# A quantised feed-forward layer, its five groups and its layernorm interleaved, with clip and maxima work moved to GpSimd

## The chip, the core and the metric

The kernel runs on one core of a Trainium2 chip. A core has five engines that run their own instruction streams and meet only at semaphores: TensorE (PE in the profile, its weight loads PEld), VectorE (DVE), ScalarE (ACT), GpSimd (POOL) and SyncE (SP, which only issues DMAs here). The metric is the time of one execution in microseconds (us); lower is better. TensorE, VectorE and ScalarE reach PSUM, the matmul accumulators of 8 banks; all engines reach SBUF.

## The reference

`x` is 16 images of 96 channels by 256 pixels. It passes, each time added to a residual, through two convolution-like attention layers (L0, L1), a causal attention (L2), a quantised feed-forward layer (`L2_ffn`), a causal attention (L3) and a mixture of experts (`L3_ffn`). The change is in the quantised feed-forward layer and in the layernorms; this is that layer:

```
h   = layernorm(x)                       # over the 96 channels of each token
y1  = h @ binarized(W1).T + b1           # 96 -> 384, weights are signs about a group mean
y1  = quantise(y1)                       # per group of 3 images
y1  = gelu(y1)
y2  = y1 @ binarized(W2).T + b2          # 384 -> 96
y2  = quantise(y2)
x   = x + y2

quantise(y), for g in range(5):          # images 3g, 3g+1, 3g+2; the 16th image stays zero
    gamma = max(abs(y[g]))               # one number over the whole group
    y[g]  = clip(y[g] * 128 / (gamma + 1e-5), -128 + 1e-5, 128 - 1e-5)
```

The scale of a group needs the maximum over all its elements, so nothing of a group can pass the gelu before the last element of its first product is there, and nothing can be added to `x` before the last of its second.

## The kernel before

Tokens are 4096, in 32 tiles of 128. `tok` holds the residual with tokens on partitions, `on` the normalised copy, `xn` the same with channels on partitions (TensorE's transposes turn one into the other, four tiles, called a chunk, at a time; 8 chunks). `big` (called `y1` here) holds the hidden layer, `ps` is PSUM. A group has 768 tokens, computed as two halves of 384.

**Layernorm** (`layer_norm` on VectorE, `norm_tail` on ScalarE, `normed_to_channels` on TensorE), used four times as `ln2`, `lnf2`, `ln3`, `lnf3`: VectorE takes statistics, ScalarE a square root, VectorE the reciprocal; then of each chunk VectorE normalises three tiles and ScalarE one (`on`), TensorE transposes the four, and ScalarE copies the result into `xn`.

**The feed-forward stage** follows an order written out by hand in three tables. `h` is the first matmul of a group (six products of 128x384, one PSUM bank each), `c` ScalarE's copies of them to `y1`, `a` VectorE's maximum of absolute values along each partition, `q` scale and clip of `y1` on VectorE, `e` the gelu on ScalarE, `y` on TensorE the second matmul and on VectorE the addition of the bias and the maximum, `f` scale, clip, addition to `tok`, and the statistics of the next layernorm. After each `a` and each `y` GpSimd takes the maximum over the partitions (`partition_all_reduce`). The first matmul starts when all eight chunks of the layernorm are in `xn`. `quant_scale` turns a maximum into a scale with three small VectorE steps, each waited for (`link`).

```
F2_PE  = ["h0", "h1", "h2", "h3", "y0", "h4", "y1", "y2", "y3", "y4"]
F2_ACT = ["c0", "c1", "c2", "e0", "c3", "e1", "c4", "e2", "e3", "e4"]
F2_DVE = ["a0", "a1", "q0", "a2", "q1", "a3", "q2", "y0", "a4", "q3", "y1", "f0", ...
```

Each engine takes its steps strictly in its table's order, so a step that waits holds up everything behind it.

Of the kernel before, what the change touches and what calls it, by code (L numbers as in the profile page):

```python
# [60 lines left out]
NORM = {"gn0": 1, "gn1": 2, "ln2": 3, "lnf2": 4, "ln3": 5, "lnf3": 6}  # L61
TURN = {"ln2": 0, "lnf2": 8, "ln3": 16, "lnf3": 24}
# [19 lines left out]
def hybrid_kernel(nc, x_d, w96_d, w128_d, out_d):  # L82
    ctx = ExitStack()
    with ctx:
# [162 lines left out]
        def _(pool):  # L247
# [30 lines left out]
            for l in (1, 2, 3):  # L278
                pool.wait_ge(sg("w96_loaded"), 16)
                if l == 1:  # L280
# [40 lines left out]
        def _(act):  # L321
# [7 lines left out]
            def norm_tail(name):  # L329

                norm_sqrt(name, P, NT)
                act.wait_ge(sg("norm_scale"), TURN[name] // 8 + 1)
                for g in range(9):
                    if g < 8:
                        t = 4 * g + 3
                        nc.scalar.activation(on[:, t, :], tok[:, t, :], ACT.Identity, bias=st[:, 6, t:t + 1],  # L336
                                             scale=st[:, 5, t:t + 1]).then_inc(sg("ln_ta"), 1)
                    if g >= 1:
                        act.wait_ge(sg("ln_t_ps"), TURN[name] + g)
                        nc.scalar.activation(xn[0:C, (g - 1) * 512:g * 512], ps[0:C, 4 + (g - 1) % 4, :], ACT.Copy).then_inc(sg("xn_copied"), 1)  # L340
# [7 lines left out]
            act.wait_ge(sg("l0_logit"), 1)  # L348
            nc.scalar.activation(aff[:, :, :], a0[:, :, :], ACT.Exp, scale=C ** -0.5).then_inc(sg("l0_exp"), 1)
            nc.scalar.activation(st[:, 5, :], st[:, 4, :], ACT.Exp, scale=-C ** -0.5).then_inc(sg("l0_exp"), 1)  # L350
            act.wait_ge(sg("l0_qkv_ps"), 1)
            nc.scalar.activation(qkv0[:, :, :], ps[0:C, 2, 0:3 * B * M].rearrange("p (a b) -> p a b", a=3), ACT.Copy).then_inc(sg("l0_qkv"), 1)
            act.wait_ge(sg("l0_sc"), 1)
            nc.scalar.activation(pr2[:, :, :, :], pr[:, :, :, :], ACT.Exp, scale=(C // H0) ** -0.5).then_inc(sg("l0_sexp"), 1)
            act.wait_ge(sg("l0_proj_ps"), 1)
            nc.scalar.activation(s64[:, 5, :], ps[0:C, 0, 0:B * M], ACT.Identity, bias=wa("l0_pb", C)).then_inc(sg("l0_stf2"), 1)
            act.wait_ge(sg("l0_stft_ps"), 1)
            nc.scalar.activation(stft[:, :], ps[0:B * M, 1, 0:C], ACT.Copy).then_inc(sg("l0_stft"), 1)
# [43 lines left out]
            for l in (1, 2, 3):  # L402
# [38 lines left out]
                if l == 2:  # L441
# [10 lines left out]
                    norm_tail("lnf2")  # L452
                    act.sem_inc(sg("f2_y1"), 6)
# [778 lines left out]
```

## Time and profile before

| | |
|---|---|
| time, median of 3 runs | 1001.02 us (998.97 to 1004.37) |
| profiled execution, first to last instruction | 1000.7 us |
| TensorE busy | 826.8 us (83%) |
| VectorE busy | 733.6 us (73%) |
| ScalarE busy | 586.7 us (59%) |
| GpSimd busy | 138.3 us (14%) |
| mean granted TensorE clock | 0.918 of full speed |
| the feed-forward stage, from its layernorm's scale to the last statistics | 554.85 to 630.49 us |

A time in the trace counts from the first instruction. The profiled execution's own time is its span, 1000.7 us; nothing lies around it in the numbers given, and it stands 0.3 us below the median of the runs. A row of the timeline gives start, length, engine, line of the kernel, operation, what is written and read, how many instructions it merges, and in brackets how long the engine had been idle and who released it. Instructions of one engine overlap a little at their ends, so the pitch from one start to the next, not the length, is what an engine spends.

### The profile page before, as it was taken

What the parts mean: (1) busy time and instruction counts of PE and PEld (TensorE: products, weight loads), DVE (VectorE), ACT (ScalarE), POOL (GpSimd) and SP (SyncE); (2) the same over time, 40 slices, a digit from 0 to 9 for tenths busy, and PEclk for the clock granted to TensorE, in tenths of its full rate; (3) what the DMA queues carried; (4) which work ended last, traced back from release to release, by engine and by line L of the source; (5) the groups of instructions that cost most, each with busy time, mean ns of one, the idle gap of its engine ahead of it and who ended that gap; (6) DMA issues with size and microseconds to landing.
All of it is one profiled execution on the core that took longest, in us unless ns stands there. A gap on an engine that the chain in (4) does not pass through costs nothing.

```text
span 1000.7 us, 19812 instructions
## 1 busy us (share of the span) xinstructions
PE 826.8 (83%) x5997; PEld 667.3 (67%) x5997; DVE 733.6 (73%) x2103; ACT 586.7 (59%) x1826; POOL 138.3 (14%) x200
## 2 busy tenths in 40 slices
PE   0875799999999466999997776489999949999996
PEld 0761566666666364778885456278788738999995
DVE  6317799999999653899998599479999972354344
ACT  0211678777777224888887652378889842444442
POOL 9002333333333000000000000000000010000000
PEclk9997899999999776999999797679999967999998
DMA  5000000000000643566664000246666600000000
GB/s 187 1 0 1 1 0 0 0 0 0 0 0 0 57 70 48 90 85 94 94 94 63 1 0 1 32 78 85 91 94 94 91 4 1 9 8 16 8 8 16
DMA packets 51260, 38.05 MB, mean 38 GB/s; under 512 B 28448, under 2 KB 43296, under 8 KB 50976
## 3 DMA queue, kind: packets, MB, share of 16 engines
q1 hardware_dynamic: 50784, 36.14, 23.8%
q0 software_dynamic: 448, 1.57, 0.6%
q8 instruction: 14, 0.23, 0.1%
q14 instruction: 14, 0.11, 0.0%
HBM read 6.24 MB, written 3.15 MB: 9 GB/s over the span
## 4 chain that ended last, share of the span: by engine, by line
PE 65%; DVE 22%; issue 5%; DMA 4%; SPq 2%; ACT 2%; DVEq 0%; ACTq 0%
PE ps L660 9%; PE ps L790 8%; PE ps L610 8%; PE ps L769 7%; PE ps L557 6%; PE ps L564 6%; DVE sqj L995 3%; PE ps L601 3%; PE ps L566 3%; DVE ee L958 2%; PE ps L574 2%; PE ps L575 2%; DVE on L856 2%; DVE chst L837 2%; DVE xn L831 2%
## 5 line engine op out<-in xcount | busy, mean ns | idle before, releaser
L380 ACT ACTIVATE ee<-ps,nmax 128x128 f32<-128x128 f32 (+1 forms) x588 | 248.9, 442 | 10.2 <-DVE nmax L917 7.7
L958 DVE TENSOR_SCALAR ee<-ee,rrec 128x128 f32<-128x128 f32 (+1 forms) x588 | 173.4, 358 | 5.2
L660 PE MATMUL ps<-w,ee 128*128 128x128 f32 x960 | 137.3, 280 | 19.7 <-DVE ee L958 19.7
L367 ACT ACTIVATE big<-ps 128x384 f32<-128x384 f32 (+1 forms) x224 | 113.3, 538 | 40.4 <-PE ps L660 39.5
L660 PEld LDWEIGHTS ps<-w,ee 128*128 128x128 f32 x960 | 104.2, 142 | 45.3 <-DVE ee L958 33.7
L380 ACT ACTIVATION_READ_ACCUMULATOR ee<-ps,nmax 128x1 f32 x588 | 124.1, 211 | 0.0
L917 DVE TENSOR_REDUCE nmax<-ps 128x2 f32<-128x256 f32 x200 | 101.1, 546 | 18.1 <-PE ps L566 18.1
L564 PE MATMUL ps<-qk 128*128 128x128 f32 (+1 forms) x400 | 103.8, 349 | 12.6 <-DMA qk<-lo 9.6
L471 ACT ACTIVATE big<-ps 128x512 f32<-128x512 f32 x96 | 57.3, 597 | 84.5 <-PE ps L769 83.2
L790 PEld LDWEIGHTS ps<-w,big 128*128 128x128 f32 x768 | 98.1, 191 | 7.1
L564 PEld LDWEIGHTS ps<-qk 128*128 128x128 f32 x400 | 79.9, 207 | 30.6 <-issue 17.1
L557 PE MATMUL ps<-kh,big 128*128 128x256 f32 x400 | 97.4, 387 | 1.6 <-ACT ee L380 1.6
L275 POOL TENSOR_TENSOR big<-qs,w 96x256 f32<-96x256 f32 x108 | 78.6, 758 | 144.6 <-ACT qs L390 144.6
L790 PE MATMUL ps<-w,big 128*128 128x96 f32 x768 | 96.3, 272 | 0.0
L610 PE MATMUL ps<-big,vh 128*32 128x256 f32 (+1 forms) x1188 | 92.4, 353 | 0.5 <-DVE big L989 0.5
L566 PE MATMUL ps<-maskb,identb 128*128 128x128 bf16 x400 | 90.4, 236 | 0.0
L769 PE MATMUL ps<-qk 128*128 128x512 f32 x288 | 88.1, 423 | 1.0 <-DVE gate L1118 1.0
L557 PEld LDWEIGHTS ps<-kh,big 128*128 128x128 f32 x400 | 74.3, 192 | 17.7 <-issue 6.2
L1152 DVE TENSOR_TENSOR big<-ps,w 128x384 f32<-128x384 f32 x32 | 15.6, 550 | 87.8 <-PE ps L790 87.8
L914 DVE TENSOR_REDUCE nmax<-ps 128x4 f32<-128x1024 f32 x50 | 60.9, 1217 | 17.4 <-PE ps L557 17.4
L269 POOL COPY xb<-xn 96x256 f32 (+1 forms) x54 | 24.8, 462 | 327.1 <-PE ps L587 277.4
L495 PE MATMUL ps<-w,on 128*96 128x128 f32 x128 | 29.9, 411 | 42.8 <-ACT on L336 27.1
(215 smaller groups left out, 1296.4 us busy)
## 6 DMA issues: line engine op xcount, KB each, us to landing
qk<-hi SPq DMA_DIRECT2D x36, 192.0 KB, 3.7
qk<-hi SPq DMA_DIRECT2D x72, 96.0 KB, 3.8
qk<-lo SPq DMA_DIRECT2D x36, 192.0 KB, 4.8
qk<-lo SPq DMA_DIRECT2D x72, 96.0 KB, 4.6
w<-w_in SPq DMA_DIRECT2D x1, 1829.5 KB, 13.9
xc<-x_in SPq DMA_DIRECT2D x4, 384.0 KB, 5.9
l_mix<-on SPq DMA_DIRECT2D x8, 192.0 KB, 6.5
tok<-l_mix POOLq DMA_DIRECT2D x4, 384.0 KB, 4.9
```

Source lines behind the costliest of these rows:

```text
L275: last = nc.gpsimd.tensor_tensor(qh[0:C, par, g, :], qs[:, :], wa("l1_hw", C)[:, g:g + 1].broadcast_to([C, N]), ALU.mult)
L367: nc.scalar.activation(et[:, h, 0:w], ps[:, 4 + hh, 0:w], ACT.Copy).then_inc(own(l, f"et{hh}"), 1)
L380: last = nc.scalar.activation(ee[:, ke, hh, qc, 0:w], src, ACT.Exp, bias=nmax[:, kp, hh, qc:qc + 1], accum_out=rsum[:, kp, hh, qc:qc + 1])
L557: last = mm(ps[:, 2 * kp + hh, qc * N:(qc + 1) * N], qh[:, par, 2 * u + hh, qc * P:(qc + 1) * P], kh[:, par, :], start=True, stop=True)
L564: mm(ps[:, 2 * kp + hh, qc * N:qc * N + w], qk[:, par, h, 0, qc * P:(qc + 1) * P], qk[:, par, h, 1, 0:w], start=True, stop=False)
L566: last = mm(ps[:, 2 * kp + hh, qc * N + qc * P:qc * N + (qc + 1) * P], identb[:, :], maskb[:, :], start=False, stop=True)
L610: last = mm(ps[32 * r:32 * (r + 1), 6, g * N + q0:(g + 1) * N], vh[:, par, tc, 3 * g + r, :], et[:, 3 * g + r, tc * N:tc * N + N - q0], st ...
L660: last = nc.tensor.transpose(ps[:, 4 + hh, b * P:(b + 1) * P], ee[:, u, hh, qc, tc * P:(tc + 1) * P], ident)
L769: last = mm(ps[:, 4 + s % 4, :], w1hl[:, w, s * P:(s + 1) * P], xhl[:, par, x, :], start=(n == 0), stop=(n == 2))
L790: last = mm(ps[:, q, e * C:(e + 1) * C], h3[:, r % 4, q * P:(q + 1) * P], wb("f3_w2")[:, r * C:(r + 1) * C], start=(j == 0), stop=(j == NJ ...
L917: last = V.tensor_reduce(out=nmax[:, kp, :, qc], in_=ps[:, 2 * kp:2 * kp + 2, qc * N:qc * N + scores_cols(l, qc)], axis=AX.X, op=ALU.max, ...
L958: last = V.tensor_scalar(v, v, rrec[:, kp, hh, qc:qc + 1], None, ALU.mult)
```

## The change

- **Tables.** `F2_PE`, `F2_ACT` and `F2_DVE` are new, and GpSimd gets one of its own, `F2_POOL`. The eight chunks of the `lnf2` layernorm are steps in them (`t` on TensorE, `m` and `x` on ScalarE), put between the half-groups of the first matmul. A half-group waits for the chunk that holds its last token. The transposes of `lnf2` use PSUM banks 6 and 7 in place of 4 to 7.
- **Scale in the gelu.** `q` no longer touches `y1`. It is one reciprocal on VectorE, and ScalarE's gelu multiplies by that scale. The gelu runs in halves.
- **Clip after the gelu**, on GpSimd (`p`), in halves, as one instruction with two operations. The second matmul waits for the clip of its half.
- **Maxima.** After each all-reduce GpSimd adds the epsilon and divides by 128 itself, a second small instruction; VectorE keeps the reciprocal.
- **Layernorm.** In `ln2`, `lnf2`, `ln3` and `lnf3` one more tile of each chunk moves, from VectorE to GpSimd (`norm_pool`): two tiles on VectorE, one on GpSimd, one on ScalarE.
- **Semaphores of layer L0** are merged into three, counted up; the order of work there is the same.

```diff
-F2_PE = ["h0", "h1", "h2", "h3", "y0", "h4", "y1", "y2", "y3", "y4"]
-F2_ACT = ["c0", "c1", "c2", "e0", "c3", "e1", "c4", "e2", "e3", "e4"]
-F2_DVE = ["a0", "a1", "q0", "a2", "q1", "a3", "q2", "y0", "a4", "q3", "y1", "f0", "q4", "y2", "f1", "y3", "f2", "y4", "f3", "f4"]
+F2_PE = ["t0", "h00", "t1", "h01", "t2", "h10", "t3", "h11", "t4", "h20", "t5", "h21", "t6", "t7",
+         "y0", "h30", "h31", "y1", "h40", "h41", "y2", "y3", "y4"]
+F2_ACT = ["m0", "m1", "x0", "c00", "m2", "x1", "c01", "m3", "x2", "c10", "m4", "x3", "c11", "m5", "x4", "e00", "e01",
+          "c20", "m6", "x5", "c21", "m7", "x6", "x7", "e10", "e11", "e20", "e21", "c30", "c31", "e30", "e31",
+          "c40", "c41", "e40", "e41"]
+F2_DVE = ["a0", "q0", "a1", "q1", "a2", "y0", "q2", "f0", "a3", "y1", "q3", "f1", "a4", "y2", "q4", "f2", "y3", "f3", "y4", "f4"]
+F2_POOL = ["a0", "p0", "a1", "p1", "a2", "y0", "p2", "a3", "y1", "p3", "a4", "y2", "p4", "y3", "y4"]
...
+            def norm_pool(name):
+
+                pool.wait_ge(sg("norm_scale"), TURN[name] // 8 + 1)
+                for g in range(8):
+                    t = 4 * g + 2
+                    nc.gpsimd.tensor_scalar(on[:, t, :], tok[:, t, :], st[:, 5, t:t + 1], st[:, 6, t:t + 1], ALU.mult, ALU.add).then_inc(sg("ln_tp"), 1)
...
+                        if step[0] == "p":
+                            for b in range(2):
+                                v = y1[:, :, g * GT + b * (GT // 2):g * GT + (b + 1) * (GT // 2)]
+                                pool.wait_ge(sg("f2_gelu"), 2 * g + b + 1)
+                                nc.gpsimd.tensor_scalar(v, v, QB - QEPS, -QB + QEPS, ALU.min, ALU.max).then_inc(sg("f2_clip"), 1)
+                        else:
...
+                            nc.gpsimd.partition_all_reduce(m, amax[:, 2 * k, g:g + 1], P, bass.bass_isa.ReduceOp.max).then_inc(sg(f"f2_gred{k}"), 1)
+                            pool.wait_ge(sg(f"f2_gred{k}"), g + 1)
+                            nc.gpsimd.tensor_scalar(m, m, QEPS, 1.0 / QB, ALU.add, ALU.mult).then_inc(sg(f"f2_gmax{k}"), 1)
...
-                            act.wait_ge(sg("f2_quant"), g + 1)
-                            nc.scalar.activation(y1[:, :, g * GT:(g + 1) * GT], y1[:, :, g * GT:(g + 1) * GT], ACT.Gelu).then_inc(sg("f2_gelu"), 1)
+                            act.wait_ge(sg("f2_scale"), g + 1)
+                            nc.scalar.activation(y1[:, :, c0:c1], y1[:, :, c0:c1], ACT.Gelu, scale=amax[:, 0, g:g + 1]).then_inc(sg("f2_gelu"), 1)
...
+                bank, banks = (6 + g % 2, 2) if name == "lnf2" else (4 + g % 4, 4)
...
+                            pe.wait_ge(sg("xn_copied"), TURN["lnf2"] + (a + GT // 2 - 1) // 512 + 1)
...
-                            pe.wait_ge(sg("f2_gelu"), g + 1)
                             for b in range(2):
+                                pe.wait_ge(sg("f2_clip"), 2 * g + b + 1)
...
-                            quant_scale(0, g)
-                            v = y1[:, :, g * GT:(g + 1) * GT]
-                            link(V.tensor_scalar(v, v, amax[:, 0, g:g + 1], QB - QEPS, ALU.mult, ALU.min))
-                            V.tensor_scalar(v, v, -QB + QEPS, None, ALU.max).then_inc(sg("f2_quant"), 1)
+                            dve.wait_ge(sg("f2_gmax0"), g + 1)
+                            V.reciprocal(amax[:, 0, g:g + 1], amax[:, 1, g:g + 1]).then_inc(sg("f2_scale"), 1)
...
-                            quant_scale(1, g)
+                            dve.wait_ge(sg("f2_gmax1"), g + 1)
+                            link(V.reciprocal(amax[:, 2, g:g + 1], amax[:, 3, g:g + 1]))
```

VectorE's rows at steps `a4 q3 y1 f0` of the kernel before: the maximum of group 4 along partitions, the three small steps and the two passes over the hidden layer of group 3 (`big`), the second layer's bias and maximum of group 1 (`on`), and the first small steps of group 0's last part.

```order
L1079 TENSOR_REDUCE amax<-big 128x1
L1071 TENSOR_SCALAR amax<-amax 128x1
L1072 RECIPROCAL amax<-amax 128x1
L1073 TENSOR_SCALAR amax<-amax 128x1
L1084 TENSOR_SCALAR big<-big,amax 128x3x768
L1085 TENSOR_SCALAR big<-big 128x3x768
L1092 TENSOR_TENSOR on<-ps,w 128x288 x2
L1095 TENSOR_REDUCE amax<-on 128x1
L1071 TENSOR_SCALAR amax<-amax 128x1
```

The same engine at steps `a3 y1 q3 f1` of the change:

```order
L1122 TENSOR_REDUCE amax<-big 128x1
L1133 TENSOR_TENSOR on<-ps,w 128x288 x2
L1136 TENSOR_REDUCE amax<-on 128x1
L1126 RECIPROCAL amax<-amax 128x1
L1140 RECIPROCAL amax<-amax 128x1
L1142 TENSOR_SCALAR on<-on,amax 128x576
L1143 SCALAR_TENSOR_TENSOR tok<-on,tok 128x576
```

The two passes over `big` are gone, and `f` of a group (L1140 on) now follows the maximum of the same group (L1136) with one reciprocal between them; before, `f` used the maximum of the group ahead.

GpSimd before, through the whole feed-forward stage:

```order
L290 COMPARE_AND_BRANCH
L316 ISA
L316 ISA amax<-amax 128x1 x10
L269 COPY xb<-xn 96x256 x2
L290 UNCONDITIONAL_BRANCH
```

GpSimd after, from the layernorm `lnf2` to step `p1` (L340 is the all-reduce, L342 the small step behind it, L335 the clip):

```order
L278 TENSOR_SCALAR on<-tok,st 128x96 x8
L340 ISA
L340 ISA amax<-amax 128x1
L342 ISA
L342 TENSOR_SCALAR amax<-amax 128x1
L335 TENSOR_SCALAR big<-big 128x3x384 x2
L340 ISA
L340 ISA amax<-amax 128x1
L342 ISA
L342 TENSOR_SCALAR amax<-amax 128x1
L335 TENSOR_SCALAR big<-big 128x3x384 x2
```

An all-reduce now stands behind the clips of another group on the same engine, and each has a second instruction behind it.

## Rows read from the trace of the kernel before

**Rows 1.** Windows: length; busy us of PE, PEld, DVE, ACT, POOL; clock; DMA

```profile
554.80:580.00 25.20, 22.86 (x79) 14.28 (x80) 14.95 (x33) 17.52 (x35) 0.73 (x2) 0.82 0.00 1
580.00:600.00 20.00, 14.49 (x86) 11.94 (x84) 19.55 (x21) 10.94 (x15) 1.40 (x4) 0.91 0.00 0
```

**Rows 2.** Timeline of VectorE in the feed-forward stage

```profile
554.85 5.85 DVE L856 TENSOR_SCALAR on<-tok,st 128x96 f32<-128x96 f32 x24
569.46 2.55 DVE L1079 TENSOR_REDUCE amax<-big 128x1 f32<-128x2304 f32 x1 [8.76 <-ACT big L460]
...
576.36 1.82 DVE L1084 TENSOR_SCALAR big<-big,amax 128x2304 f32<-128x2304 f32 x1
578.21 1.76 DVE L1085 TENSOR_SCALAR big<-big 128x2304 f32<-128x2304 f32 x1
579.89 2.54 DVE L1079 TENSOR_REDUCE amax<-big 128x1 f32<-128x2304 f32 x1
...
601.04 0.81 DVE L1092 TENSOR_TENSOR on<-ps,w 128x288 f32<-128x288 f32 x2
601.88 0.75 DVE L1095 TENSOR_REDUCE amax<-on 128x1 f32<-128x576 f32 x1
602.55 0.14 DVE L1071 TENSOR_SCALAR amax<-amax 128x1 f32<-128x1 f32 x1
...
603.12 0.52 DVE L1100 TENSOR_SCALAR on<-on,amax 128x576 f32<-128x576 f32 x1
...
606.11 0.15 DVE L1071 TENSOR_SCALAR amax<-amax 128x1 f32<-128x1 f32 x1
...
622.26 0.75 DVE L1095 TENSOR_REDUCE amax<-on 128x1 f32<-128x576 f32 x1
...
626.48 0.15 DVE L1071 TENSOR_SCALAR amax<-amax 128x1 f32<-128x1 f32 x1
...
630.49 0.18 DVE L848 TENSOR_SCALAR st<-chmv 128x32 f32<-128x32 f32 x1
```

**Rows 3.** Timeline of ScalarE in the same stage

```profile
577.18 1.28 ACT L464 ACT_TABLE_LOAD   x1
580.00 2.12 ACT L464 ACTIVATE big<-big 128x2304 f32<-128x2304 f32 x1 [1.54 <-DVE big L1085]
582.03 2.38 ACT L460 ACTIVATE big<-ps 128x384 f32<-128x384 f32 x6
```

**Rows 4.** Timeline of TensorE in the same stage (a matmul is two records)

```profile
555.72 1.94 PE L495 MATMUL ps<-w,on 128*96 128x128 f32 x8 [9.65 <-ACT on L336]
...
564.76 15.75 PE L740 MATMUL ps<-xn,w 128*128 128x384 f32 x48 [0.68 <-ACT xn L340]
582.27 4.23 PE L753 MATMUL ps<-w,big 128*128 128x96 f32 x36 [1.76 <-ACT big L464]
...
601.63 7.38 PE L753 MATMUL ps<-w,big 128*128 128x96 f32 x36 [2.21 <-DVE on L1092]
```

**Rows 5.** Window inside the last of these rows, columns as Rows 1

```profile
602.00:604.00 2.00, 2.00 (x11) 2.00 (x11) 1.86 (x6) 1.28 (x1) 0.35 (x1) 0.50 0.03 8
```

**Rows 6.** Timeline of GpSimd, its nearest operations

```profile
572.15 0.38 POOL L316 PARTITION_ALL_REDUCE amax<-amax  x1 [41.83 <-DVE amax L1079]
...
802.63 1.46 POOL L308 CAST qk<-w 128x1536 fp32r<-128x1536 f32 x1 [13.66 <-DMA qk<-lo]
811.56 2.89 POOL L310 TENSOR_TENSOR qk<-w,qk 128x1536 fp32r<-128x1536 f32 x1 [7.47 <-issue]
```

**Rows 7.** Timeline of VectorE and GpSimd where they work together

```profile
811.53 2.99 DVE L856 TENSOR_SCALAR on<-tok,st 128x96 f32<-128x96 f32 x1
...
142.48 1.14 DVE L958 TENSOR_SCALAR ee<-ee,rrec 128x256 f32<-128x256 f32 x4
...
144.54 4.45 POOL L275 TENSOR_TENSOR big<-qs,w 96x256 f32<-96x256 f32 x6 [8.63 <-ACT qs L390]
...
147.41 2.12 DVE L958 TENSOR_SCALAR ee<-ee,rrec 128x256 f32<-128x256 f32 x4
```

More of the change, by code:

```diff
@@ L485, in group_sums, with normed_chunk @@
                 mm(ps[0:C, 0, B:2 * B], wb("avg3", C), st[0:C, 1, 0:B], start=True, stop=True).then_inc(sg("gn_vg"), 1)
+            def normed_chunk(name, g):
+                bank, banks = (6 + g % 2, 2) if name == "lnf2" else (4 + g % 4, 4)
+                pe.wait_ge(sg("ln_tn"), TURN[name] + g + 1)
+                pe.wait_ge(sg("ln_tp"), TURN[name] + g + 1)
+                pe.wait_ge(sg("ln_ta"), TURN[name] + g + 1)
+                if g >= banks:
+                    pe.wait_ge(sg("xn_copied"), TURN[name] + g - banks + 1)
+                for t in range(4):
+                    last = nc.tensor.transpose(ps[0:C, bank, t * P:(t + 1) * P], on[:, g * 4 + t, :], ident)
+                last.then_inc(sg("ln_t_ps"), 1)
             def normed_to_channels(name):
                 for g in range(8):
[L490 to L496 removed]
+                    normed_chunk(name, g)
             pe.wait_ge(sg("w128_loaded"), 16)
@@ L734, in _ @@
                         g = int(step[1])
-                        if step[0] == "h":
-                            for b in range(2):
-                                for j in range(NJ):
-                                    a = g * GT + b * (GT // 2)
-                                    pe.wait_ge(sg("f2_y1"), g * 6 + (b * NJ + j + 1))
-                                    mm(ps[:, b * NJ + j, 0:GT // 2], wa("f2_w1")[:, j * P:(j + 1) * P], xn[:, a:a + GT // 2],
-                                       start=True, stop=True).then_inc(sg("f2_y1_ps"), 1)
+                        if step[0] == "t":
+                            normed_chunk("lnf2", g)
+                        elif step[0] == "h":
+                            b = int(step[2])
+                            a = g * GT + b * (GT // 2)
+                            pe.wait_ge(sg("xn_copied"), TURN["lnf2"] + (a + GT // 2 - 1) // 512 + 1)
+                            for j in range(NJ):
+                                pe.wait_ge(sg("f2_y1"), g * 6 + (b * NJ + j + 1))
+                                mm(ps[:, b * NJ + j, 0:GT // 2], wa("f2_w1")[:, j * P:(j + 1) * P], xn[:, a:a + GT // 2],
+                                   start=True, stop=True).then_inc(sg("f2_y1_ps"), 1)
                         else:
@@ L854, in layer_norm @@
                 for g in range(8):
-                    for t in range(4 * g, 4 * g + 3):
+                    for t in range(4 * g, 4 * g + 2):
                         last = V.tensor_scalar(on[:, t, :], tok[:, t, :], st[:, 5, t:t + 1], st[:, 6, t:t + 1], ALU.mult, ALU.add)
```

151 lines of the change are left out of this document (77 added, 74 removed).

## The prediction, made before the changed kernel was run

> **What bounds the kernel now.** I read the page first: TensorE is busy most, but the chain that ended last passes through both TensorE and VectorE, and the change touches one stage, so I went to that stage's timeline. It starts at 554.85, when the layernorm's scale is ready and VectorE begins on its 24 tiles, and ends at 630.49, when the statistics of the next layernorm are done [rows 2]: 75.6 us. Outside it the change only moves one tile per chunk in three other layernorms. The reader should see three things. First, from 554.8 to 580 VectorE is busy 14.95 of 25.2 us, and one wait of 8.76 us before the first maximum is most of the rest [rows 1, 2]; TensorE is busy 22.86 us of the same stretch, at a mean clock of 0.82. Second, from 580 on VectorE is the engine that never stops, 19.55 of 20 us [rows 1], while TensorE waits for it [rows 4]. Third, GpSimd does next to nothing here, 1.40 us of those 20.
>
> So the stage splits at the start of the third maximum, `a2`, at 579.89 [rows 2]: before it TensorE's feed of hidden-layer products sets the pace, behind it VectorE's own work, 50.6 us of it. I work out the two parts apart.
>
> **First part, up to `a2`.** The interleaving lets TensorE begin the first matmul after one chunk instead of eight. What that brings depends on the clock. Before, TensorE starts its transposes at 555.72, eight of them in 1.94 us, 0.24 each [rows 4]; when the first matmul starts at 564.76 it takes 15.75/24 = 0.66 us per product of 384 columns. The mean clock of 0.82 over the stretch, against the two levels of 0.5 and 1.0, says that the first 9 us of it ran at the lower level, 1.2 GHz. The new order puts products of twice 0.66 = 1.3 us into these 9 us. From 555.7: chunk 0 (four transposes) 0.96, its copy with two signals 0.8, `h00` 3.9, chunk 1 0.96, its copy 0.8, one product of `h01` 1.3, together 8.7, which is 564.4. Then at the full clock: two products 1.3, chunk 2 0.6, its copy 0.8, `h10` 2.0, chunk 3 0.6, `h11` 2.0, which ends at about 571.6, and its last copy at 572.2. Copies are 2.38/6 = 0.40 us per 384 columns [rows 3], so about 0.5 for a chunk of 512. From there ScalarE's table is the chain: tile and copy (`m5`, `x4`) 0.9, the table load of 1.28, two half gelus of 1.2 each (half of 2.12 and 0.14 more for the second start), `c20` 1.2, `m6` and `x5` 0.9, `c21` 1.2 [rows 3], together 7.9. So `a2` starts at 580.1, 0.2 us later than before. The early start is spent on the lower clock and on the table load and gelu that now stand ahead of group 2's copies. What is ahead, though, is the work behind: `q0` and `q1` no longer cost VectorE anything that it has not idle time for.
>
> **Second part, from `a2` on.** VectorE's pitches before [rows 2]: `a` 2.45, `y` 601.04 to 602.55 = 1.51, three small steps 602.55 to 603.12 = 0.57, `f` without them 603.12 to 606.11 = 2.99 (0.45 more for the last, of eight tiles), `q` 0.57 + 1.85 + 1.68 = 4.1. Three `a` 7.4, four `q` 16.4, five `y` 7.6, five `f` with small steps 17.8 + 0.45, waits 1.0: 50.6, which is the trace. After: 7.4, three reciprocals at 0.2 = 0.6, 7.6, and five `f` with one reciprocal 16.0 + 0.45, together 32.0. That takes off 18.6 us. Four things give some back:
>
> - **The second layer of group 0 (3.0 us).** `y0` follows `a2` at 582.5 at once, but TensorE can only start it at about 581.9, after the last chunk's copy, and needs 4.23 for it [rows 4]; VectorE waits until about 586.2, 0.4 of which is its own addition. I take 3.0; at 1.8 for a half it would be 2.6.
> - **Round trips of the maxima (4.9 us).** Before, another step always lay between a maximum and its use. Now `q` stands right behind, and `f` one reciprocal behind. A round trip is a signal to GpSimd (a maximum ending at 572.01 releases it at 572.15: 0.14), the all-reduce (0.35 to 0.38), a signal, the small step, a signal. I take the small step no longer than the all-reduce, so 3 x 0.14 + 2 x 0.35 = 1.1 us [rows 2, 6]. It is seen five times, three of them with 0.2 of reciprocal over it: 3 x 0.9 + 2 x 1.1 = 4.9. Queued behind VectorE's wait is all the rest of the stage. The trace bounds the trip from above only loosely: from the maximum ending at 623.01 to its use at 626.48, 3.47 us [rows 2].
> - **GpSimd and VectorE in each other's way (4.2 us).** A VectorE tile that took 0.24 in pitch elsewhere took 2.99 us when a GpSimd operation of 2.89 us ran beside it, until that ended; four others took 2.12 instead of 1.14 [rows 6, 7]. So GpSimd holds VectorE's SBUF-to-SBUF `tensor_scalar` for its own length. `f0`, `f1` and `f2` have such an instruction (0.52) and one that reads two SBUF operands, and the clips of groups 2, 3 and 4 fall beside them: a clip follows the gelu that follows `q`, and `f` follows `q` too. A clip is 128x1152. At the cast's rate, 1.46/1536, it is 1.1 us; at that of the two-operand operation, 2.89/1536, 2.2 [rows 6]. It has one tensor operand, as the cast, and two operations, so I take 1.4. One clip per `f` in the way: 3 x 1.4 = 4.2.
> - **TensorE at the lower clock (1.3 us).** After gaps of some 4 us, a group's second layer took 7.38 in place of 4.23 us at a clock of 0.50 [rows 4, 5]. `y3` and `y4` get such gaps ahead of them. Most of `y3` hides under `f2`; of `y4` one slow half less cover remains, 1.3.
>
> Together 13.4. The second part falls by 18.6 - 13.4 = 5.2.
>
> The Trainium skill, "SBUF — State Buffer", section "Who interferes with whom", says that GpSimd shares one pair of SBUF ports with VectorE as an exclusive lock held for a whole instruction, taken by VectorE's two-port modes and, for reads, by its instructions with two SBUF inputs. Rows 7 agree for the two-port case; by the rule the addition into `tok` is held as well, which the trace does not show alone. By that rule at its hardest, both of a group's clips would hold `f`, 8.4 us in place of 4.2.
>
> **The layernorm tiles, nothing (0.3 either way, each of four).** VectorE needs 5.85/24 = 0.24 per tile; a chunk of three costs it 0.73, of two 0.49. TensorE takes 0.97 per chunk plus its waits, so it is the slower, and VectorE's saving is under it [rows 2, 4]. A GpSimd tile of 96 columns costs between nothing measurable and 0.4, and even if both take turns a chunk is ready in 0.9. Without that cover, a GpSimd tile over 0.6, each layernorm loses some 8 x 0.1. In `lnf3` the tiles queue behind the 2.89 us operation of rows 6, which holds VectorE there already. The merged semaphores of L0 wait for the same things in the same order: nothing.
>
> **Sum.** First part +0.2, second part -5.2: the profiled 1000.7 becomes 995.7, the median 1001.0 becomes 996.0.
>
> **The rivals.**
>
> - *GpSimd is cheap.* The casts and copies come near this; nothing holds `f`, because the clips slip into `f`'s statistics, and a round trip is 0.8. It gives back 4.2 + 1.5 more: 990.3. Against it stand rows 7.
> - *The round trip is long (slower).* The 0.35 us of an all-reduce is one engine's record; before, no one waited for it within 3.47 us [rows 2, 6], so nothing shows what it costs a waiter. Each further us costs five exposures at `f`, and the two all-reduces that stand ahead of each of three clips on GpSimd push these into `f` as well: 8 us per us. It decides at 1.1 + 5.0/8 = 1.7 us; at 2.6 the time is 1008, at the bound of 3.47 it is 1015. "Perfetto Trace Analysis" of the Trainium skill, section "GPSIMD Engine Instruction", says that such spans are not to be trusted and that one should go by spacing; here the spacing is silent up to 3.47.
> - *The gain is eaten on GpSimd (no change).* GpSimd's operation at 811.56 had been idle for 7.47 us while VectorE ran its statistics, though its input was ready at 804.1 [rows 6]. If statistics keep GpSimd out, three clips wait 1.3 us each for the end of `f`, and with a clip of 2.2 us in place of 1.4 three more times 0.8 is lost: together 6.3, which gives 1002; one of the two alone gives 998.4 to 1000.
> - *The early start pays after all.* If TensorE reached its full clock 4 us sooner, with matmuls in place of transposes, the first part would shrink by 2 us: 994.
>
> The Trainium skill's "GPSIMD Engine Reference", section "Engine selection", advises against elementwise work on GpSimd, about twice as slow with two inputs and near VectorE's rate with one. Rows 6 show both, 1.88 and 0.95 ns per element; the clip is of the second kind.
>
> **Chances.** My forecast with the early-start variant, 992 to 999: 0.50, of which 0.29 lies more than 0.5% (5 us, about what a measurement of this kernel tells from no change) below the median. Cheap GpSimd: 0.15. Eaten gain, 998 to 1004: 0.14. Long round trip: 0.21, of which 0.18 is slower by over 0.5%. Faster: 0.29 + 0.15 = 0.44. Slower: 0.18 and 0.02 for a clip and a trip both dear. The rest, 0.36, is within 0.5%. The range takes in the cheap case with 2 us for a better first part, 988, and reaches to a round trip of about 2.6, 1008.
>
> **What would show it.** Each step has its row: `a2`'s start near 580 (first part); VectorE's idle time before the reciprocals of L1126 and L1140, 0.9 to 1.1 us each (round trip); L1142 or L1143 at 1.5 us or more with a clip beside it (hold); L335 near 1.4 us; the second layers of groups 3 and 4 at a clock of 0.5; unchanged starts of the first transposes after the layernorms. I am wrong if L1126 and L1140 wait 2 us, if L335 is over 2 us, or if `a2` starts before 577.

## The result, and the profile after

The changed kernel takes 1088.58 us, median of 4 runs (1086.16 to 1090.9); the kernel before, on the same chip, 1001.01 (998.97 to 1004.37). The ratio is 1.0867, 95% interval 1.084 to 1.0894: 87.6 us slower, where the prediction had 5 us faster and a range that ended at 1008. The profiled execution took 1088.56 us, with a span of 1086.5.

Almost all of it is in the feed-forward stage. It now runs from 555.37 to 716.98 us, 161.6 us, where it took 75.6 [rows 2]: 86.0 us more. The windows of the stage after, with the columns of [rows 1], say at once which kind of loss it is:

```profile
554.80:580.00 25.20, 17.11 (x60) 10.07 (x60) 9.62 (x21) 15.82 (x31) 6.63 (x12) 0.84 0.00 0
580.00:600.00 20.00, 16.43 (x92) 13.58 (x92) 4.10 (x5) 5.30 (x9) 2.85 (x4) 0.80 0.00 1
600.00:717.00 117.00, 26.62 (x121) 22.91 (x120) 32.04 (x97) 13.03 (x19) 11.84 (x22) 0.58 0.00 0
```

From 600 on no engine is busy more than 28% of the time: VectorE 32.04 of 117 us, TensorE 26.62, GpSimd 11.84. VectorE never stopped before (19.55 of 20 us); now it stands idle most of the time. So no engine's work is the limit: the engines wait for something that is not the length of an instruction. The waits of VectorE (engine, what waits, for whom: us in total, times, the longest) name it:

```profile
DVE amax L1140 <- POOL amax L342: 59.2, 5, 13.6
DVE amax L1126 <- POOL amax L342: 49.7, 5, 14.3
```

These are the two uses of a maximum, the scale of `f` (L1140) and that of the gelu (L1126). Ten waits hold 108.9 us. The prediction counted five of them as seen, 0.9 to 1.1 us each, 4.9 us together. The waits of GpSimd itself:

```profile
POOL amax L342 <- issue: 71.2, 10, 7.9
...
POOL amax L340 <- issue: 47.0, 8, 6.0
```

"issue" is idle time in which the engine waited for no other engine that the profile shows. GpSimd's timeline shows where in the work of a group it lies (L340 is the all-reduce, L342 the small step on its result, L335 the clips):

```profile
568.43 0.38 POOL L340 PARTITION_ALL_REDUCE amax<-amax  x1 [9.22 <-DVE amax L1122]
575.57 0.18 POOL L342 TENSOR_SCALAR amax<-amax 128x1 f32<-128x1 f32 x1 [6.75 <-issue]
577.32 2.29 POOL L335 TENSOR_SCALAR big<-big 128x1152 f32<-128x1152 f32 x2 [1.57 <-ACT big L507]
585.30 0.38 POOL L340 PARTITION_ALL_REDUCE amax<-amax  x1 [5.69 <-issue]
592.46 0.18 POOL L342 TENSOR_SCALAR amax<-amax 128x1 f32<-128x1 f32 x1 [6.79 <-issue]
...
624.01 0.18 POOL L342 TENSOR_SCALAR amax<-amax 128x1 f32<-128x1 f32 x1 [7.21 <-issue]
624.27 2.46 POOL L335 TENSOR_SCALAR big<-big 128x1152 f32<-128x1152 f32 x2
```

```profile
632.65 0.38 POOL L340 PARTITION_ALL_REDUCE amax<-amax  x1 [5.92 <-issue]
640.23 0.18 POOL L342 TENSOR_SCALAR amax<-amax 128x1 f32<-128x1 f32 x1 [7.21 <-issue]
646.16 0.38 POOL L340 PARTITION_ALL_REDUCE amax<-amax  x1 [5.75 <-issue]
653.42 0.18 POOL L342 TENSOR_SCALAR amax<-amax 128x1 f32<-128x1 f32 x1 [6.88 <-issue]
653.68 2.46 POOL L335 TENSOR_SCALAR big<-big 128x1152 f32<-128x1152 f32 x2
```

The small step of 0.18 us starts 7 us after the all-reduce of 0.38 whose result it takes. The next all-reduce starts 6 us after the `tensor_scalar` ahead of it. Between one clip and that of the next group (624.27 to 653.68, 29.4 us) these four gaps are 5.92 + 7.21 + 5.75 + 6.88 = 25.8 us. Two `tensor_scalar` in a row (L342, then L335 at 624.27) have no gap. A passage from the all-reduce to `tensor_scalar` or back is called a turn from here on. What lies in the gaps shows when one asks for everything that is recorded on a line, the small step's line L342 here (operation, count, shortest/median/longest ns, first and last start):

```profile
L342 POOLq MODIFY_POOL_CONFIG  x20: 82/83/83, 568.8 to 705.9; - x20
L342 POOL TENSOR_SCALAR amax<-amax x10: 181/181/182, 575.6 to 713.1; 128x1 f32<-128x1 f32 x10
```

Ten `tensor_scalar` and, in GpSimd's queue, a `MODIFY_POOL_CONFIG` ahead of each (two records for each), the first at 568.8, as soon as the all-reduce is done. L340 has 20 such records as well. This is the nameless `ISA` row that stands ahead of each L340 and each L342 in the order shown with the change; before, the whole stage had one.

VectorE's timeline after, to be read against [rows 2]:

```profile
575.78 0.16 DVE L1126 RECIPROCAL amax<-amax 128x1 f32<-128x1 f32 x1 [7.48 <-POOL amax L342]
575.86 2.53 DVE L1122 TENSOR_REDUCE amax<-big 128x1 f32<-128x2304 f32 x1
592.68 0.16 DVE L1126 RECIPROCAL amax<-amax 128x1 f32<-128x1 f32 x1 [14.28 <-POOL amax L342]
592.76 2.53 DVE L1122 TENSOR_REDUCE amax<-big 128x1 f32<-128x2304 f32 x1
...
624.22 0.16 DVE L1140 RECIPROCAL amax<-amax 128x1 f32<-128x1 f32 x1 [13.64 <-POOL amax L342]
624.42 1.31 DVE L1142 TENSOR_SCALAR on<-on,amax 128x576 f32<-128x576 f32 x1
625.76 1.58 DVE L1143 SCALAR_TENSOR_TENSOR tok<-on,tok 128x576 f32<-128x576 f32 x1
```

`a2` starts at 592.76 instead of 580.1, behind the first two long waits. A wait that has both turns in it, into the all-reduce and out of it, is 13.0 to 14.3 us.

**Theories, stated before the experiments.** Theory 1: GpSimd has to load other code whenever it goes from the all-reduce to `tensor_scalar` or back, 6 to 7 us each time, and nothing else matters. The rivals: the all-reduce's result reaches a waiter late, some 7 us, whatever follows it; or GpSimd is overloaded or held out by VectorE, having clips and maxima in one in-order queue. The expectations below number them theories 2 and 3; neither gives a price to a small GpSimd instruction that nobody waits for.

### The profile page after: what moved, and what is told of

Same layout as the page of the kernel before. It is cut to its first block, busy times and chain, and to the rows that moved or that the text cites. A ratio compares the mean times of both kernels' runs of the same rounds, so it can differ in the third digit from the quotient of the medians.

```text
span 1086.5 us, 19879 instructions
## 1 busy us (share of the span) xinstructions
PE 831.3 (77%) x5997; PEld 669.1 (62%) x5997; DVE 708.9 (65%) x2041; ACT 587.0 (54%) x1831; POOL 167.5 (15%) x252
## 4 chain that ended last, share of the span: by engine, by line
PE 59%; DVE 16%; issue 14%; DMA 4%; ACT 2%; SPq 2%; POOL 1%; DVEq 0%; POOLq 0%; ACTq 0%
PE ps L709 8%; PE ps L841 8%; PE ps L659 7%; PE ps L820 7%; PE ps L606 6%; PE ps L613 5%; DVE sqj L1046 3%; PE ps L650 2%; PE ps L615 2%; DVE ee L1009 2%; DMA qk<-lo 2%; PE ps L623 2%; PE ps L624 2%; DVE xn L882 2%; SPq L236 1%
## 5 line engine op out<-in xcount | busy, mean ns | idle before, releaser
L709 PEld LDWEIGHTS ps<-w,ee 128*128 128x128 f32 x960 | 104.1, 142 | 45.4 <-DVE ee L1009 33.5
L841 PE MATMUL ps<-w,big 128*128 128x96 f32 x768 | 96.4, 272 | 0.0
L804 PE MATMUL ps<-w,big 128*128 128x96 f32 x180 | 30.3, 348 | 57.6 <-DVE on L1133 56.7
L539 PE MATMUL ps<-w,on 128*96 128x128 f32 x128 | 27.0, 368 | 57.7 <-POOL on L278 39.1
```

The source lines that it names most:

```text
L709: last = nc.tensor.transpose(ps[:, 4 + hh, b * P:(b + 1) * P], ee[:, u, hh, qc, tc * P:(tc + 1) * P], ident)
L841: last = mm(ps[:, q, e * C:(e + 1) * C], h3[:, r % 4, q * P:(q + 1) * P], wb("f3_w2")[:, r * C:(r + 1) * C], start=(j == 0), stop=(j == NJ ...
```

## The experiments

In each batch the kernel before ran on the same chip; the ratio is to that, over all runs, and can differ a little from the quotient of the two medians. Each diff is cut to the lines that matter.

**1. Half the turns.** The small step goes back to VectorE, so that a group has two turns (into its maxima, back to its clips) in place of four.

```diff
-    nc.gpsimd.partition_all_reduce(...).then_inc(sg(f"f2_gred{k}"), 1)
-    pool.wait_ge(sg(f"f2_gred{k}"), g + 1)
-    nc.gpsimd.tensor_scalar(m, m, QEPS, 1.0 / QB, ALU.add, ALU.mult).then_inc(sg(f"f2_gmax{k}"), 1)
+    nc.gpsimd.partition_all_reduce(...).then_inc(sg(f"f2_gmax{k}"), 1)
 (VectorE, "q" and ahead of "f")
+    link(V.tensor_scalar(m, m, QEPS, 1.0 / QB, ALU.add, ALU.mult))
```

> The changed kernel, with the small step behind each all-reduce given back to VectorE; the clips stay on GpSimd. Theory 1 (GpSimd must load other code whenever it goes from an all-reduce to a tensor_scalar or back, about 6 to 7 us each, seen as a pool-configuration row and idle time with the releaser issue): the turns in the feed-forward stage fall from 20 to 10, a period of one group falls from 29 to some 17 us, and the time to 1015 to 1040. Theory 2 (an all-reduce itself takes 7 us to finish, whatever stands beside it): all ten remain and the time stays above 1075. Theory 3 (the new order of steps makes engines wait, GpSimd's code is no part of it): within 5 us of 1088.

Measured: 1028.71 us (1028.16 to 1036.02), ratio 1.0277 (1.0234 to 1.032). Two thirds of the loss (59.9 of 87.6 us) went. GpSimd's queue has twelve loads where the change has twenty: two in place of four in each group, and the last one ahead of the tiles of `ln3`. What is left stands where it did, now ahead of the clip:

```profile
584.81 0.38 POOL L340 PARTITION_ALL_REDUCE amax<-amax  x1 [5.82 <-issue]
592.34 2.25 POOL L335 TENSOR_SCALAR big<-big 128x1152 f32<-128x1152 f32 x2 [7.15 <-issue]
```

**2. No turns inside the groups.** In addition the clips are on VectorE (steps `p`), so that GpSimd does all-reduces alone; the interleaving of the groups, the gelu's scale and the layernorm tiles stay.

```diff
-F2_POOL = ["a0", "p0", "a1", "p1", "a2", "y0", "p2", ...]
+F2_POOL = ["a0", "a1", "a2", "y0", "a3", "y1", "a4", "y2", "y3", "y4"]
-F2_DVE = ["a0", "q0", "a1", "q1", "a2", "y0", "q2", "f0", ...]
+F2_DVE = ["a0", "q0", "a1", "q1", "p0", "a2", "p1", "y0", "q2", "f0", "p2", ...]
```

> As the first, and the clips go to VectorE too, with steps p in its table; GpSimd does nothing but all-reduces between the layernorm and the next. Interleaving, scale inside the gelu and moved layernorm tiles stay. Theory 1: no turn is left inside the stage, waits of VectorE for GpSimd fall under 1.5 us, and the stage takes 55 to 68 us in place of 161.6: 982 to 996. Theory 2: ten all-reduces of 7 us, most of them waited for: above 1040. Theory 3: the order is kept, so the time stays near 1080.

Measured: 1002.97 us (999.48 to 1005.89) against 1003.06, ratio 1.0004 (0.9988 to 1.0021). The loss is gone, but the gain that was expected did not come: the range was 982 to 996. In GpSimd's timeline one turn is left, from the last all-reduce to the layernorm tile of `ln3`:

```profile
621.96 0.35 POOL L340 PARTITION_ALL_REDUCE amax<-amax  x1 [5.11 <-DVE amax L1140]
629.43 3.62 POOL L278 TENSOR_SCALAR on<-tok,st 128x96 f32<-128x96 f32 x8 [7.11 <-issue]
```

VectorE's tiles of this layernorm started at 627.26, so GpSimd's came 2.2 us behind them, and TensorE's first transpose started at 630.02, 2.76 us behind them. Experiment 5 takes this up.

**3 and 4. The turn alone.** To the kernel before, with its order and its engines, one GpSimd instruction of 128x1 on unused memory is added behind each all-reduce. Nobody waits for it. In one kernel it is a `tensor_scalar`, in the other a `tensor_copy`.

```diff
     nc.gpsimd.partition_all_reduce(...).then_inc(sg(f"f2_gmax{k}"), 1)
+    nc.gpsimd.tensor_scalar(junk[:, x:x + 1], junk[:, 0:1], 1.0, 1.0, ALU.add, ALU.mult)   # 3
+    nc.gpsimd.tensor_copy(junk[:, x:x + 1], junk[:, 0:1])                                  # 4
```

> The kernel before, with one tensor_scalar of 128x1 on GpSimd added behind each all-reduce, on a column that nothing else uses and nobody waits for. Theory 1: ten more turns each way, about 13 us from one all-reduce to the next where 2.5 to 9.2 us were, and the stage grows by 60 to 80 us: 1060 to 1085. Theories 2 and 3: no change, 999 to 1004, since nothing waits for the new operation.

> The kernel before, with a tensor_copy of 128x1 in the place of that tensor_scalar. In both traces copies follow an all-reduce or a tensor_tensor without a pool-configuration row. Theory 1: copies belong to the code that is always there, so no change: 999 to 1004. If any other operation between two all-reduces costs the turn, 1060 to 1085 as with the tensor_scalar.

Measured: with the `tensor_scalar` 1068.04 us (1066.04 to 1068.74), ratio 1.0639 (1.0616 to 1.0661); with the copy 1002.84 (998.41 to 1005.36), ratio 0.9996 (0.998 to 1.0012). Ten instructions of 0.18 us that nobody needs cost 65 us, ten of 0.25 us nothing. GpSimd's timelines, the `tensor_scalar` first:

```profile
571.63 0.38 POOL L316 PARTITION_ALL_REDUCE amax<-amax  x1 [41.63 <-DVE amax L1080]
579.16 0.18 POOL L318 TENSOR_SCALAR junk<-junk 128x1 f32<-128x1 f32 x1 [7.15 <-issue]
585.41 0.38 POOL L316 PARTITION_ALL_REDUCE amax<-amax  x1 [6.06 <-issue]
```

```profile
568.38 0.38 POOL L316 PARTITION_ALL_REDUCE amax<-amax  x1 [41.73 <-DVE amax L1080]
568.65 0.25 POOL L318 COPY junk<-junk 128x1 f32<-128x1 f32 x1
572.22 0.35 POOL L316 PARTITION_ALL_REDUCE amax<-amax  x1 [3.32 <-DVE amax L1080]
```

GpSimd has hardly more work than before in either kernel, and nearly the same in both, so overload falls with the pair. A late result of the all-reduce can't be it either: nobody waits for one here, and where VectorE waits for it directly, in experiment 2, it is idle for 0.22 to 0.55 us. Nor is it GpSimd's wait on its own semaphore between the two instructions, which the change added: experiment 3 has no such wait and the same gap, experiment 7 has the wait and no gap. What the runs show is that the gap depends on the kinds of the two instructions; that it is code being loaded is read from the record's name.

**5. The last turn out of the way.** Experiment 2 with the third tile of `ln3` back on VectorE, and the turn taken by a `tensor_scalar` for which nobody waits, in the idle time behind the last all-reduce.

```diff
-                if l > 1:
-                    norm_pool(f"ln{l}")
+                if l == 2:
+                    norm_pool("ln2")
+                if l == 3:
+                    nc.gpsimd.tensor_scalar(junk[:, 250:251], wb("mask")[:, 0:1], 1.0, 1.0, ALU.mult, ALU.mult)
 (VectorE)
-                    for t in range(4 * g, 4 * g + 2):
+                    for t in range(4 * g, 4 * g + (3 if name == "ln3" else 2)):
```

> The maxima-only version (clips and small steps on VectorE, one all-reduce kind on GpSimd) with the third layernorm tile of every chunk of ln3 back on VectorE, so that no GpSimd instruction stands between the last all-reduce and TensorE's first transpose. One tensor_scalar of 128x1 that nobody waits for takes the load for the tiles of lnf3 in the idle time behind it. Theory 1 (loading GpSimd's code on each change between all-reduce and tensor_scalar): the wait of TensorE on L278, which ended 2.2 us behind the scale, goes, and the time falls by about 2 us against the maxima-only version, to 999 to 1001.5. Rival (the gain of the interleaving is lost elsewhere, in the colder clock of TensorE after the stage): no change against it, 1002 to 1004.

Measured: 997.5 us (996.03 to 999.27) against 1003.7, ratio 0.995 (0.993 to 0.997), somewhat better than expected and the fastest complete kernel of the study. GpSimd's timeline behind the last all-reduce:

```profile
621.49 0.35 POOL L343 PARTITION_ALL_REDUCE amax<-amax  x1 [5.10 <-DVE amax L1143]
628.53 0.19 POOL L298 TENSOR_SCALAR junk<-w 128x1 f32<-128x1 f32 x1 [6.69 <-issue]
```

The gap is the same 7 us, but TensorE's transposes start at 627.65, 0.86 us behind the start of VectorE's tiles (626.79) in place of 2.76. That is 1.9 us for the turn. The medians of experiments 2 and 5 lie 5.5 us apart, and the other 3.6 are not shown to come from it: the two ran in different batches, and the parts of the kernel that no edit touches move by as much. The kernel before and experiments 3, 4 and 10, the same code up to there, started the stage's tiles between 551.2 and 554.9. From the first tile of `lnf2` to that of `ln3` this kernel's trace has 75.1 us, experiment 2's 71.7 and the kernel before 76.7, so what the interleaving itself gains, 1.6 to 5.0 us by these traces, is uncertain too.

**6. No clips.** Experiment 1 without the clip of the gelu's result.

```diff
-                                nc.gpsimd.tensor_scalar(v, v, QB - QEPS, -QB + QEPS, ALU.min, ALU.max).then_inc(sg("f2_clip"), 1)
 (TensorE)
-                                pe.wait_ge(sg("f2_clip"), 2 * g + b + 1)
+                                pe.wait_ge(sg("f2_gelu"), 2 * g + b + 1)
```

> The changed kernel with the small step on VectorE and without the clip of the gelu's result (left out), so GpSimd does all-reduces alone from group 0 to the last. Theory 1: no turn of code lies inside the groups any more, so nothing waits for GpSimd beyond 0.6 us, VectorE does 32 us of work behind a2 plus waits of about 6 us for the second layer of group 0 and the round trips, and the last turn costs 2 us at ln3: 986 to 994. Rival (the all-reduce's round trip itself is long when VectorE waits at once for it, 3 us or more each): 1005 to 1015.

Measured: 998.9 us (996.27 to 1003.81), ratio 0.9964 (0.9946 to 0.9983). The rival's 1005 to 1015 is out, but the expectation of 986 to 994 was missed too. It had counted VectorE's work and left out that VectorE waits for ScalarE in each of groups 3 and 4 (1.26 us); experiment 7 shows the same loop more clearly. The turn ahead of `ln3`, which was expected, is there (GpSimd idle for 7.00 us).

**7. The change with one kind of code.** Every all-reduce is replaced by a `tensor_scalar`; nothing else is touched. The kernel leaves out the maximum over the partitions.

```diff
-                            nc.gpsimd.partition_all_reduce(m, amax[:, 2 * k, g:g + 1], P, bass.bass_isa.ReduceOp.max).then_inc(...)
+                            nc.gpsimd.tensor_scalar(m, amax[:, 2 * k, g:g + 1], 1.0, 1.0, ALU.mult, ALU.mult).then_inc(...)
```

> The changed kernel with every all-reduce of the two maxima replaced by a tensor_scalar of 128x1, which leaves out the maximum over the partitions; clips, small steps, waits, steps and their order are those of the change. All of GpSimd's work in the stage is now of one kind. Theory 1: no loads at all, the idle time ahead of L342 and of the replaced instruction falls from 6 to 8 us to under 0.3, and the whole loss goes: 988 to 1000, where the prediction had 996; a clip of 1.2 us with an f beside it still holds VectorE's tensor_scalar for some 0.8 us twice a group. Rival (GpSimd's in-order queue of 15 steps with clips ahead of reductions is a good part of the loss, whatever its code): 1015 or more.

Measured: 993.85 us (992.95 to 994.19) against 1003.7, ratio 0.9906 (0.9882 to 0.9929). All clips, small steps, waits and orders of the change are in it, and it is 9.9 us faster than before instead of 87.6 slower. GpSimd's timeline, the same places as in the changed kernel above:

```profile
578.15 0.19 POOL L340 TENSOR_SCALAR amax<-amax 128x1 f32<-128x1 f32 x1
578.43 0.19 POOL L342 TENSOR_SCALAR amax<-amax 128x1 f32<-128x1 f32 x1
583.62 2.29 POOL L335 TENSOR_SCALAR big<-big 128x1152 f32<-128x1152 f32 x2 [5.00 <-ACT big L507]
...
592.83 2.77 POOL L335 TENSOR_SCALAR big<-big 128x1152 f32<-128x1152 f32 x2 [0.89 <-ACT big L507]
```

No "issue" time is left. This kernel also lets the other terms of the prediction be read one by one, below.

**8. The layernorm tiles alone.** The kernel before with the third tile of each chunk on GpSimd (`norm_pool`, and its wait on TensorE), nothing else.

> The kernel before with one part of the change alone: the third layernorm tile of every chunk on GpSimd. Theory 1: three turns of code come with it. The one ahead of the first all-reduce and the one between the last all-reduce and ln3 fall into idle time (6.8 us from the last all-reduce to the scale in the kernel before, against a load of 7), so at most 1 us is lost there; in lnf3 the code is loaded already for the subtraction behind it, which starts earlier and no longer holds the tiles of VectorE, 2.5 us gained: 998 to 1001.5, against 1001 to 1003 for the kernel before. Rival (elementwise work on GpSimd slows the layernorms): 1003 to 1008, half a us or more lost in each of four.

Measured: 1000.61 us (999.36 to 1003.33) against 1003.7, ratio 0.9982 (0.9967 to 0.9997), as expected: 3.1 us faster by the medians, 1.8 by the ratio. The subtraction follows its cast at once (805.41 behind 803.86), and the tiles of `ln3` on GpSimd end their wait with the scale, not with "issue".

**9. Bound inside the scale.** Experiment 6 made into a complete kernel, with the `ln3` arrangement of experiment 5. In place of the clip, the 128x1 scale is bounded, by one small VectorE instruction more in each group, so that no scaled value passes 128 - eps.

```diff
+                            link(V.tensor_scalar(amax[:, 0, g:g + 1], amax[:, 1, g:g + 1], QEPS, 1.0 / QB, ALU.add, ALU.mult))
+                            link(V.scalar_tensor_tensor(out=amax[:, 1, g:g + 1], in0=amax[:, 1, g:g + 1], scalar=1.0 / (QB - QEPS), in1=amax[:, 0, g:g + 1], op0=ALU.mult, op1=ALU.max))
```

> The version without clips, small step on VectorE, made into a full kernel: the bound that the clip kept is put into the 128x1 scale (the greater of (m + eps)/128 and m/(128 - eps) is inverted, so no scaled value passes 128 - eps), and the third layernorm tile of ln3 is on VectorE with the load for lnf3 taken behind the last all-reduce, as in e5. Theory 1 (turns of code) with TensorE as the pace of the groups: against e6 the wait for the last turn, 2 us, and the slowed tiles of VectorE beside it, 1 us, go: 995 to 997, below e5's 997.5 by 0.5 to 2, since a group takes 9.1 us with TensorE as the pace and 9.6 with VectorE. Rival (VectorE and TensorE alternate so tightly that one 128x1 instruction more per group shows each time): 997 to 999, no better than e5.

Measured: 998.96 us (995.02 to 1000.86) against 1002.64, ratio 0.9963 (0.9947 to 0.9979): not better than experiment 5, as the rival had it. A group takes 9.33 us (594.67 to 604.00) in its trace, against 9.14 in experiment 6 and 9.63 in experiment 5: the small instruction shows its 0.19 us in each. The expectation took TensorE for the pace; in the trace VectorE waits for ScalarE (1.41 us a group). What keeps the time up beyond that stays open; the expected 0.5 to 2 us are within the spread of its runs.

**10. The turn taken early, in the kernel before.** One `tensor_scalar` of 128x1 behind the last all-reduce, for which nobody waits.

```diff
         (behind the loop over the all-reduces)
+                    nc.gpsimd.tensor_scalar(junk[:, 250:251], wb("mask")[:, 0:1], 1.0, 1.0, ALU.mult, ALU.mult)
```

> The kernel before with one instruction more: a tensor_scalar of 128x1 on GpSimd behind the last all-reduce, for which nobody waits. Theory 1: it takes the load of GpSimd's code in idle time (the next work of GpSimd comes 18 us later), so the subtraction that follows the cast near 803 starts at once instead of 7.5 us later and no longer lies beside the 24 layernorm tiles of lnf3, which take 5.8 us in place of 8.5: 2 to 3 us faster than the kernel before, and no MODIFY_POOL_CONFIG idle time ahead of the subtraction. Rival (the 7.5 us are GpSimd held out by VectorE's statistics, as the prediction read them): nothing changes.

Measured: 999.48 us (997.02 to 1001.34) against 1002.64, ratio 0.9977 (0.9964 to 0.9991): one useless instruction gains 3.2 us by the medians, 2.3 by the ratio. The subtraction of [rows 6] follows its cast at once, and VectorE's 24 tiles take 5.84 us where they took 8.51 before (and one of them 2.99, [rows 7]):

```profile
798.62 1.46 POOL L308 CAST qk<-w 128x1536 fp32r<-128x1536 f32 x1 [13.81 <-DMA qk<-lo]
800.17 2.90 POOL L310 TENSOR_TENSOR qk<-w,qk 128x1536 fp32r<-128x1536 f32 x1
```

```profile
798.69 5.21 DVE L838 BATCH_NORM_STATS2 chst<-tok 128x6 f32<-128x96 f32 x32
...
807.28 5.84 DVE L857 TENSOR_SCALAR on<-tok,st 128x96 f32<-128x96 f32 x24
```

The subtraction now lies wholly beside VectorE's statistics, and neither is delayed: 2.90 us against 2.89 before, and 5.21 against 5.20.

## Why the prediction was wrong

**The step that failed** is the second of the four that give back: "Round trips of the maxima (4.9 us)". It took the small step to follow the all-reduce by a signal, 1.1 us for a whole round trip. In the changed kernel the ten waits were 108.9 us, because a load of code stands between the two instructions and another between a `tensor_scalar` and the next all-reduce. The direction was in the text as the slower rival, "the round trip is long", but priced from the wrong row: it was capped at 3.47 us, the shortest time that a user had left it before, which bounds an all-reduce with nothing behind it, not the pair. The mechanism that decided was nowhere in the prediction.

**The row that had it** was in the rows all the same, and was read wrongly. GpSimd's subtraction of [rows 6] sat idle for 7.47 us ending in "issue" with its input ready. The prediction gave that to VectorE's statistics, as part of the rival "the gain is eaten on GpSimd". Two things were at hand against it. "issue" means that no other engine released it. And the records of that line in the kernel before hold the load itself, at the very end of the cast:

```profile
L310 POOLq MODIFY_POOL_CONFIG  x2: 10/10/10, 804.1 to 804.1; - x2
L310 POOL TENSOR_TENSOR qk<-w,qk x1: 2893/2893/2893, 811.6 to 811.6; 128x1536 fp32r<-128x1536 f32 x1
```

Experiment 10 settles it: with one `tensor_scalar` earlier the 7.47 us are gone while the statistics are as they were. The kernel before had three such records: this one, one into the all-reduce at 530.3, hidden in 41.83 us of idle time, and one at 95.0 ahead of its first `tensor_tensor`, which started 1.9 us later. So the record alone isn't the price. The one row with nothing else to wait for had it, though, before the run: 7.5 us, to be set against each new `ISA` row of the order.

```profile
L275 POOLq MODIFY_POOL_CONFIG  x2: 5/5/5, 95.0 to 95.0; - x2
```

The Trainium skill, "GPSIMD Engine Reference", section "Instruction dispatch", says that the first call of freshly loaded code costs GpSimd about 6 us (5.95) with no instruction to be seen for it. This case is near that size, 5.7 to 6.2 us on the way to the all-reduce and 6.7 to 7.9 us on the way back. An estimate by that page's figure gives the twenty loads of the changed kernel 20 x 5.95 = 119 us of GpSimd's time. The measured idle time is 71.2 + 47.0 = 118.2 us for eighteen of them, 6.6 each; of the other two, one left 5.80 us of idle time and one is hidden in 9.22. The prediction had not weighed that rule.

**The other steps**, read in experiment 7, which loads no code in the stage:

- *First part: right.* `a2` started at 579.97 there and at 580.11 in experiment 2; predicted 580.1.
- *VectorE's work of the second part, 32.0 us: right.* From `a2` to the last statistics it took 45.0 us (579.97 to 624.97), and its idle time in it adds up to 12.8: 32.2 of work. The prediction had 13.4 of giving back in all, so 45.4. The sum came out right by luck, with its terms off both ways:
- *Second layer of group 0, 3.0 predicted: 7.2.* VectorE waited 4.36 and 2.81 us for it. TensorE did it at the lower clock:

```profile
582.64 7.47 PE L804 MATMUL ps<-w,big 128*128 128x96 f32 x36 [0.88 <-ACT xn L365]
```

```profile
583.00:589.00 6.00, 6.00 (x30) 6.00 (x30) 0.46 (x1) 1.68 (x2) 2.67 (x4) 0.50 0.00 0
590.00:604.00 14.00, 14.00 (x82) 10.82 (x82) 11.34 (x38) 8.23 (x14) 6.13 (x10) 1.00 0.01 1
```

  The windows (columns as in [rows 1]) show a clock of 0.50 while it ran, after a stretch of single transposes with 1.5 to 2.1 us gaps, and 1.00 right behind. The prediction took the full clock's 4.23 [rows 4] there, and looked for the lower one only in groups 3 and 4.
- *TensorE at the lower clock ahead of the end, 1.3 predicted: 0.7*, the one wait of VectorE in `y3`.
- *Round trips without a turn, 4.9 predicted: 2.7.* VectorE's idle time before L1140 was 0.51 (three times) and 0.58 (twice) us, and nothing before L1126 from group 2 on. With true all-reduces, which VectorE uses itself in experiments 2 and 5, it was 0.22 to 0.55.
- *GpSimd and VectorE in each other's way, 4.2 predicted: 0 there, real in the changed kernel.* Clips that started just ahead of L1142 made it 1.31 us and L1143 1.58 in place of 0.52 and 0.76, 1.6 us in each of three groups. In experiment 7 the clips were released at 592.8, when L1142 was over and L1143 had begun: L1143 kept its 0.76 us, and the two clips took 2.77 instead of 2.29. So the mechanism is as [rows 7] had it, but in these rows the one that starts first keeps its time and the other pays. The Trainium skill, "SBUF — State Buffer", section "Who interferes with whom", states this too, and its case of two SBUF inputs, which no row of before showed alone, agrees with these rows of L1143.
- *The clip, 1.4 us predicted: 1.15*, the median of the ten (longest 1.66), near the 1.10 that the cast's rate gives.
- *Not predicted: 2.3 us of a loop through ScalarE.* VectorE's maximum `a` waited 1.15 us for ScalarE in each of groups 3 and 4:

```profile
591.50 2.40 ACT L507 ACTIVATE big<-big,amax 128x1152 f32<-128x1152 f32 x2 [6.82 <-DVE amax L1126]
593.80 2.37 ACT L504 ACTIVATE big<-ps 128x384 f32<-128x384 f32 x6
```

  In ScalarE's table the gelus stand ahead of the next copies. So scale, two gelus, six copies, `a`, `y`, next scale is a loop: 0.19 + 2.30 + 2.47 + 2.47 + 1.52 = 8.95 us by the pitches, and the period is 8.95 (591.31 to 600.26). So leaving the clips out (experiment 6, a period of 9.14) gained only half a us a group over putting them on VectorE (experiment 5, 9.63, VectorE full). The same wait stands in the traces of experiments 6 and 9, but no run tried another order on ScalarE, so this is read from traces and not shown by an experiment.
- *Layernorm tiles, nothing: nearly right.* Experiment 8 gains 1.8 to 3.1 us, which by its trace comes through the turn that goes away ahead of the subtraction in `lnf3`, as in experiment 10.

So the forecast describes the change without its loads, and the loads are the whole loss. It is less exact than 996.0 beside 993.85 looks: the kernel before took 1003.7 in that batch, so the gain is 9.9 us where 5.0 was forecast. By the traces the stage gave 6.0 of it (70.7 us against 76.7 from the first tile of `lnf2` to that of `ln3`), and 3.4 lie behind the scale of `lnf3`, where the forecast had nothing and where the turn ahead of the subtraction is gone. Undone part by part: twenty loads 1088.58, twelve 1028.71, none inside the groups but one ahead of `ln3` that is waited for 1002.97, none that is waited for 997.5.

## What to carry to other kernels

Before moving anything to GpSimd, list its instructions in order and mark where it goes from the all-reduce to `tensor_scalar` or `tensor_tensor` and back; each such place cost 5.7 to 7.9 us of that engine here, however small the instruction, and copies and casts were free of it. Keep one kind in a loop; where a turn can't be avoided, take it early with an instruction that nobody waits for, in time that is idle anyway. Idle time that ends in "issue" is no other engine's doing: ask for all the records of that line before giving it a cause, and price a new pair of instructions from a row that has the pair.

## What the runs showed of the hardware that was not expected

The load is paid in both directions and again at each turn: 5.7 to 6.2 us ahead of the all-reduce, 6.7 to 7.9 ahead of a `tensor_scalar` or `tensor_tensor` (twenty in the changed kernel, twenty in experiment 3). `tensor_scalar` and `tensor_tensor` share their code: in experiments 5, 8 and 10 the subtraction needed no load after a `tensor_scalar`, with COPY and CAST between. GpSimd's own DMA issues seem to end this: in the changed kernel four of them stand between the last `tensor_tensor` of layer L1 (324.0) and the first `tensor_scalar` of `ln2` (374.2), and a `MODIFY_POOL_CONFIG` stands at 360.4, right behind the last of them. Its price is hidden in 13.80 us of idle time, and no run shows it. The load begins when the instruction ahead ends, not when the next one's input is ready, so it hides behind a wait: in the kernel before it was recorded at 530.3, and the all-reduce started at 572.15, 0.14 us behind the maximum that it waited for. A `tensor_copy` behind an all-reduce starts at once (0.25 us), and the next all-reduce too.
